# Local layers: constant products issued by TensorE ahead of its waits in the last two passes of the loop

## The reference

```python
for i in range(DEPTH):                       # 6
    x = attn_layer(shift_tokens(x), Wqkv[i], q_scale[i], k_scale[i], Wo[i]) + x
    x = ffn_layer(shift_tokens(x), ln_g[i], ln_b[i], W1[i], b1[i], W2[i], b2[i]) + x
...
def attn_layer(x, Wqkv, qs, ksc, Wo):
    q, k, v = jnp.split(x @ Wqkv, 3, -1)     # 16 heads of 64
    q, k = l2norm(q) * qs, l2norm(k) * ksc   # then rotary
    out = local_attention(q, k, v)           # windows of 32, a window sees itself and the one before
    return out @ Wo
...
def ffn_layer(x, g, bln, W1, b1, W2, b2):
    xn = (x - mu) / jnp.sqrt(var + 1e-05) * g + bln
    a, gate = jnp.split(xn @ W1 + b1, 2, -1)
    return a * gelu(gate) @ W2 + b2
```

## Time and profile before

| | |
|---|---|
| timed runs | 2578.30, 2578.42, 2579.17 us; median 2578.42 us |
| profiled execution | 2573.15 us, span 2571.3 us |
| mean granted TensorE clock | 0.947 |
| TensorE products, span share | 2266.1 us, 88% |
| DVE, ACT, POOL | 1967.9 us (77%), 1751.1 us (68%), 1514.7 us (59%) |

### The profile page before, as it was taken

One profiled execution on the slowest core, in us unless ns is written; L12 is line 12 of the kernel. 1 busy time (PEld: TensorE's weight loads), 2 busy tenths in 40 slices (PEclk: granted clock), 3 DMA queues, 4 the chain that ended last, 5 costly groups with the idle time before them and its releaser, 6 DMA issues.

```text
span 2571.3 us, 92052 instructions
## 1 busy us (share of the span) xinstructions
PE 2266.1 (88%) x34908; PEld 1601.9 (62%) x34908; DVE 1967.9 (77%) x3232; ACT 1751.1 (68%) x3580; POOL 1514.7 (59%) x1116
## 2 busy tenths in 40 slices
PE   6999749965377777699999999999999999999995
PEld 4666438844243443367777777777777777777774
DVE  6888555543288887778888888888888888888883
ACT  4777614432366775678877888887787888888773
POOL 2666343422244444667777777777777777777770
PEclk9999979987688998899999999999999999999997
DMA  9300016903200000011221121112111211121111
GB/s 318 92 0 0 22 56 192 270 27 94 95 1 1 0 0 1 18 34 33 61 52 43 33 57 49 33 33 57 49 40 41 65 41 33 35 63 41 33 33 34
DMA packets 128651, 140.05 MB, mean 54 GB/s; under 512 B 10240, under 2 KB 96704, under 8 KB 127552
## 3 DMA queue, kind: packets, MB, share of 16 engines
q1 hardware_dynamic: 124480, 130.69, 18.4%
q0 software_dynamic: 4096, 8.40, 1.1%
HBM read 59.89 MB, written 27.26 MB: 34 GB/s over the span
## 4 chain that ended last, share of the span: by engine, by line
PE 55%; issue 2%; PEld 1%; DVE 1%; ACT 0%; PEldq 0%; POOL 0%; POOLq 0%; DVEq 0%; ACTq 0%
PE ps L2114 13%; PE ps L2125 7%; PE ps L2157 6%; PE ps L2209 6%; PE ps L2178 5%; PE ps L2235 5%; PE ps L2146 5%; PE ps L2168 3%; PE ps L2244 3%; PE ps L2138 1%; PE ps L2224 1%; PE ps L2217 1%; DVE tab L2560 0%; PEld ps L2209 0%; PEld ps L2178 0%
## 5 line engine op out<-in xcount | busy, mean ns | idle before, releaser
L2512 POOL TENSOR_TENSOR c<-a,bq 128x1024 f32<-128x1024 f32 x192 | 454.6, 2368 | 238.1 <-DVE bq L2609 237.8
L2522 POOL TENSOR_TENSOR qn<-c,ss 128x1024 f32<-128x1024 f32 x192 | 378.2, 1970 | 28.4 <-issue 3.7
L2114 PE MATMUL ps<-wqk,xs 128*128 128x512 f32 x768 | 373.0, 609 | 10.1 <-POOL xs L2505 8.2
L2608 DVE TENSOR_TENSOR a<-ps,tab 128x512 f32<-128x512 f32 x384 | 263.1, 685 | 11.2 <-ACT sq L2319 6.0
L2609 DVE TENSOR_TENSOR bq<-ps,tab 128x512 f32<-128x512 f32 x384 | 261.6, 681 | 0.0
L1575 POOL TENSOR_TENSOR hC<-hs,Cs 128x1024 f32<-128x1024 f32 x64 | 150.2, 2352 | 176.0 <-ACT Cs L1727 88.3
L2530 POOL TENSOR_TENSOR z<-z,sm 128x1024 f32<-128x1024 f32 x96 | 182.7, 1903 | 119.4 <-DVE sm L2637 119.4
L2616 DVE TENSOR_REDUCE ss<-sq 128x16 f32<-128x1024 f32 x192 | 230.2, 1217 | 27.3 <-issue 15.7
L2319 ACT ACTIVATE sq<-ps 128x512 f32<-128x512 f32 x384 | 215.3, 596 | 36.1 <-PE ps L2114 36.0
L2114 PEld LDWEIGHTS ps<-wqk,xs 128*128 128x128 f32 x768 | 140.7, 193 | 136.3 <-issue 129.8
L2125 PEld LDWEIGHTS ps<-ident,qn 128*128 128x128 f32 x1536 | 177.2, 141 | 67.7 <-issue 47.5
(11 more groups left out here) (352 smaller groups left out, 5302.8 us busy)
## 6 DMA issues: line engine op xcount, KB each, us to landing
Vw<-Vs SPq DMA_DIRECT2D x192, 256.0 KB, 4.3
win_rows<-rows_q SPq DMA_DIRECT2D x24, 256.0 KB, 3.4
outs_q<-win_out SPq DMA_DIRECT2D x24, 256.0 KB, 2.4
wqk<-in_wqkv SPq DMA_DIRECT2D x6, 1024.0 KB, 5.0
leaves<-in_q_w SPq DMA_DIRECT2D x1, 4608.0 KB, 20.6
leaves<-in_k_w SPq DMA_DIRECT2D x1, 4608.0 KB, 16.0
leaves<-in_v_w SPq DMA_DIRECT2D x8, 576.0 KB, 6.2
leaves<-in_f_w SPq DMA_DIRECT2D x8, 576.0 KB
```

The source lines that it names most:

```text
L2114: nc.tensor.matmul(jobs.out(n), xs[:, t * 128:(t + 1) * 128], wqk[:, (2 * y + s) * 512:(2 * y + s + 1) * 512], start=True, stop=True).then ...
L2512: nc.gpsimd.tensor_tensor(f(c), f(a), f(bq), ALU.add).then_inc(c_ready.sem, 1)
L2522: nc.gpsimd.tensor_tensor(qn[:, t, y, :, :, :].rearrange("p h s e -> p h (s e)"), c[:, y, :, :, :].rearrange("p h s e -> p h (s e)"), spre ...
L2608: nc.vector.tensor_tensor(a[:, y, :, s, :], Zs, spread(table(0, s), H1), ALU.mult)
```

## The change

A helper `spin(times)` issues so many products of the two constants, weights `ident_b`, 512 columns of `wmask_b`, into bank 2, each with `start` and `stop`. No semaphore is raised and nothing reads them. It is called in seven places, for passes 48 (`late and not front`, with `mid`) and 49 (`not mid`) alone. In pass 48 the second call has a wait ahead of it until `T10.1`, the last user of bank 2, has been read.

```diff
@@ -2245,6 +2245,12 @@
                                                 start=(c_ == 0), stop=(c_ == FC - 1))
                     last.then_inc(jobs.sem_filled("OUT2"), 1)
 
+                def spin(times):
+
+                    for _ in range(times):
+                        nc.tensor.matmul(core.banks.ps[:, 2, :], ident_b[:, :], wmask_b[:, :, :].rearrange("p m k -> p (m k)"),
+                                         start=True, stop=True)
+
                 def normalise():
 
                     bank = lambda b: core.banks.ps[:, b, :]
@@ -2274,14 +2280,24 @@
                     do(front, pair("Z01"), project, 0, 1)
                     if begin:
                         normalise()
+                    if late and not front:
+                        spin(8)
                     do(mid, pair("T11"), turn, m, 1, 1)
                     do(late, ("WO",), outputs, n)
                     do(mid, pair("T10"), turn, m, 1, 0)
                     do(mid, pair("P0"), turn_weights, m, 0)
+                    if late and not mid:
+                        spin(5)
                     do(late, ("mean",), mean, n)
                     do(mid, pair("S1"), scores, 1)
                     do(front, pair("T00"), turn, it, 0, 0)
+                    if late and not mid:
+                        spin(5)
                     do(late, ("var",), variance, n)
+                    if late and not front:
+                        if mid:
+                            pe.wait_ge(*jobs.taken(it, "T10.1"))
+                        spin(20 if mid else 16)
                     if front:
                         pe.wait_ge(values_ok, it + 1)
                     if begin:
```

## The result

The changed kernel took 2587.15 us (median of six runs, 2584.85 to 2589.60) against 2578.06 us for the kernel before in the same comparison (six runs, 2572.90 to 2579.17): ratio 1.004, 95% interval 1.0027 to 1.0053. It is slower, by 9.1 us on the medians, where +8.8 was forecast; the ratio compares the means, which are 10.5 us apart. The profiled execution took 2586.43 us, span 2584.6 us.

A forecast was written before the change was run, and what follows sets the result against it. The last passes were taken as bound by TensorE's own semaphore queue and half-clock stretches. Pass 48 +2.5 and pass 49 +6.3 gave +8.8 us, 2587.2 us; own range 2583.6 to 2591, 8 in 10 within 2582.5 to 2593.

The forecast's parts named there:

- The bound: Last pass: most waits end with TensorE's own queue of `skip` semaphore instructions, about 0.15 us each, not with DVE or ACT.
- Price: One added product of 512 columns: 0.22 us at full clock, 0.43 us at half.
- Pass 48: The 28 products added in `it` = 48: +2.5 us together.
- The eight ahead of `T11`: Pass 48: take 3.4 us at half clock, but `T11` and `WO` then run at full clock: zero.
- The twenty: Pass 48, behind the variance: semaphore work waits for them, `P1` starts 2.1 us later, clock falls anyway, +0.4 more.
- Pass 49: The 42 products added in `it` = 49: six terms summing to +6.3 us.
- the variance's own -0.6: Pass 49: the variance product itself runs at full clock, -0.6 us, leaving +0.5 with the products ahead of it.
- the five products ahead of it: Pass 49, before the variance product: stand in the path in full, +1.1 us.
- the eight products ahead of `OUT2`: Pass 49: in the path because semaphores were last; from +0.7 to +3.4 us, taken as +2.5.
- The full clock throughout: Rival: clock stays at full from the first added product on; total +0.7 us, 2579.1 us; chance 0.13.
- Cheap semaphore instructions: Rival: semaphore instructions nearly free in timed runs, added products lie in data waits; -6.6 us, 2571.8 us; chance 0.05.
- Half clock in the whole last pass: Rival: added products run at half clock throughout pass 49; +20.6 us with pass 48, 2599 us; chance 0.12.

The follow-up runs named there:

- e_lean: Kernel before with less semaphore work in passes 48 and 49 and no added product; ratio 0.9973 (0.9958 to 0.9988).
- e_behind: Changed kernel with the twenty and the sixteen products moved behind the semaphore work, right before `P1` and the hidden products; ratio 1.0033 (1.0019 to 1.0047).
- a_third: Unchanged copy of the changed kernel, a third look at its last stretch; no timed ratio of its own is given.
- a_again: Unchanged copy of the changed kernel, timed again; median 2589.90 us in six runs, ratio 1.0065 (1.0048 to 1.0082) to the kernel before.
- e_wo8: Kernel before with only the eight products ahead of `WO` of pass 49 added; ratio 1.0001 (0.9987 to 1.0015).
- e_lean_spin: `e_lean` with constant products fitted into the waits for data in passes 48 and 49; ratio 0.9961 (0.9947 to 0.9976).
- e_p20: Changed kernel with only the twenty products behind the variance of pass 48 kept; ratio 1.0014 (1.0002 to 1.0026).
- e_no16: Changed kernel without the sixteen products behind the variance of pass 49; ratio 1.0029 (1.0011 to 1.0047).
- e_best: `e_lean_spin` with one batch of additions moved behind the gating and seven products ahead of pass 48's values; ratio 0.996 (0.9947 to 0.9973), median 2562.55 us.

## Why the prediction was right, step by step

Each step as a piece of the last stretch, from TensorE's timelines; before is the mean of three profiles, after of four (means of numbers that agree within 0.2 us but for those marked).

| piece | before | after | difference | forecast |
|---|---|---|---|---|
| `OUT2` of pass 47 to variance of pass 48 | 18.3 (17.8 to 18.7) | 18.6 | +0.3 | 0 |
| variance to `P1` | 6.69 | 8.74 | +2.05 | +2.1 |
| `P1` to values | 6.93 | 7.40 (6.6 to 7.7) | +0.5 | +0.4 |
| values of pass 49 to end of `WO` | 11.11 | 8.70 | -2.4 | -2.1 |
| end of `WO` to `mean` | 1.66 | 2.51 | +0.85 | +1.1 |
| `mean` to end of variance | 3.06 (2.9 to 3.4) | 3.65 | +0.6 | +0.5 |
| end of variance to hidden products | 4.44 | 7.82 | +3.4 | +3.5 |
| hidden products | 4.56 | 5.22 (4.5 to 5.5) | +0.7 | +0.8 |
| their end to the end of `OUT2` | 4.83 | 5.59 (5.2 to 6.9) | +0.75 | +2.5 |
| the two pieces left | 8.65 | 8.62 | 0 | 0 |
| sum | 70.3 | 76.9 | +6.6 | +8.8 |

- **The bound.** That TensorE's own queue was last ahead of nearly every group of the last pass was right: `e_lean` took that work away and the last stretch lost 8.6 us.
- **Price.** The 16 took 3.62 us, 0.22 to 0.23 each; over a group that met both levels of the clock `e_behind` shows 0.34 us a product, and at half clock the 8 at the start of pass 48 took 3.38, 0.42 each.
- **Pass 48.** The eight ahead of `T11` took their 3.4 us at half clock, and the clock rose ahead of `T11` (1.04 us) and `WO` (3.62): zero, as forecast. The twenty cost the semaphores' 2.05 us in full, and the clock fell behind them.
- **Pass 49.** Five of its six pieces are within 0.3 us of their terms. One of the five is partly luck: the variance's own -0.6 was read from its 1.19 us in the first profile, but in both copies of before it took 0.67, so nothing was to be won there in them; the five products ahead of it cost less than the +1.1 that I gave them. The term that was mis-sized is the eight products ahead of `OUT2`, "nearer the half-clock end, +2.5": in three profiles of four the clock had risen by then, the eight took 1.89 us and `OUT2` 1.46, +0.3 together; only in `a_third` did they take 2.77 and 2.31, +2.0.
- **The agreement of the total.** That +8.8 forecast and +9.1 measured lie so close is luck. The profiles place +6.6 in the pieces that the sum is made of, so the sum was 2.2 us too high, 1.75 of it at `OUT2`. The other 2.5 us of the 9.1, and much more in `a_again`, lie in nothing that the sum has a term for: in the one profiled execution of that comparison what goes beyond the last stretch stands ahead of it, where the time spreads by 8 us with the same code, and for the executions without a profile the place is open.
- **The rivals.** The full clock throughout falls: it is at half in three places, for the first eight added products and behind the two long rows of semaphore instructions. The trace agrees with the Trainium skill's rule that I had set beside it, that activity releases the throttle (TensorE: Matmul & The Clock Gate, Part 1: The HAM clock gate), with its 27 us at 1.00; the rule says nothing against the three places. Cheap semaphore instructions fall: `e_lean`, which adds no product and takes most of them away, is faster in the timed runs too (0.9973), and the changed kernel and every part of it are on the side that dear ones give or show nothing (1.0001 for `e_wo8`). Half clock in the whole last pass falls. The Trainium skill's 131 ns a product (same page, Back-to-back issue gap) is not seen in any row here: 0.21 us is the least.

## What to carry to other kernels

Ask which queue ends each wait before filling it. Here TensorE's waits of the last pass were its own bookkeeping, semaphore instructions of 0.15 us each behind a drain, and work put ahead of a drain adds to them in full; taking the bookkeeping away gained about 7 us in the timed runs (3 to 11), putting products ahead of it cost 9. Products that only keep TensorE busy cost nothing where the wait is for data and they end before the data come, as four of the five groups in pass 49 of `e_lean_spin` show; they brought the products behind them to full clock, though the 1.2 us that the stretch lost by it is too little to be seen in the timed runs. With a long idle piece between them and the work they did nothing for the clock (the sixteen), and behind one they ran in part at half clock themselves (6.53 us for the twenty).

## What the runs showed that I had not expected

- TensorE stood still with nothing named for 1.1 to 2.2 us at single places of straight-line code: behind 110 of the 128 values' products (1.12 us in the changed kernel; 1.13 in before, 2.16 in pass 49 of `e_p20`), behind one weight load (1.35 us in `e_wo8`). Whether it happened, and where, changed from kernel to kernel; what it is, no run here tells.
- The stop within the values of pass 48 bears on the clock. Twelve of the fourteen profiles have it (1.11 to 1.68 us), and in eleven of these the products that follow run at half clock, at least in part; in `e_no16` it stayed up behind a stop of 1.39 us. In the two without it, `e_wo8` and `e_best`, the clock stayed at full. That the stop brings the clock down is likely by this, not shown. The piece up to the first variance took 14.5 and 15.5 us without the stop and 17.3 to 20.5 with it, a difference as large as what the sixteen products cost.
- The same code ahead of pass 47's `OUT2` spread over 2500 to 2508 us between executions, while the four last stretches of the changed kernel lay within 0.3 us of one another.
